# The residual add of a fused attention and fp8-linear block, moved from GpSimd's arithmetic to an accumulating DMA

## The chip, the cores and the metric

The kernel runs on one core of a Trainium2 chip. The metric is the device time in microseconds, the median of three runs; lower is better. The engines are TensorE (PE in the profile; PEld its weight loads), VectorE (DVE), ScalarE (ACT), GpSimd (POOL) and SyncE (SP), which here only issues DMAs.

## What is computed

The input x is 8 x 2048 x 512, in fp32. Attention runs over the first axis: each of the 2048 positions is a batch entry of its own with 8 tokens, 16 heads of 32.

```
xn   = layernorm(x)                                 # over the last axis
q, k, v = xn @ Wqkv.T + bqkv
attn = softmax(mask + scale * q k^T) v @ Wproj.T + bproj
lin  = fp16(fp8(xn)) @ fp16(fp8(Wffn)).T + bffn     # rounded to fp8 first
out  = x + attn + lin
```

The mask blocks keys so that queries 0 to 3 see keys 0 to 3 alone, and queries 4 to 7 see all eight.

## The kernel before

The rows are cut into 128 tiles of 128 positions x 512 numbers: tile t is token t % 8 of one half of a block of positions. Eight tiles in a row share one set of keys and values. Tiles with t % 8 below 4 are light (four keys), the others heavy (eight keys). The work is a pipeline written out by hand: in slot s each engine does stage L of tile s - L, with the stage numbers in one list (L_NORM = 3, L_KV = 4, L_Q = 5, L_QK = 8, L_SOFT = 10, L_PV = 11, L_SUM = 12, L_SPLIT = 13, L_LIN = 14, L_PROJ = 15). Each engine runs its own stream in order; semaphores alone tie the streams. The last ten tiles or so are written out apart, in `ending()` of each engine.

What each engine does in a slot, in its order, as far as the change touches it:

- PE: projection of tile s-15 into `proj_ps` (L942, then twelve matmuls of L909), the fp8 linear of s-14 (L951), the keys, values and queries of s-4 and s-5 (L909, twelve matmuls each). That is 53 matmuls. The keys wait for the transposed tile `xT`.
- DVE: statistics of a freshly loaded x (L1235), the sum of the weighted values `o_nat` (L1244), which waits for POOL's products, then query times keys (L1151), its reduction (L1156), the softmax sum and its reciprocal (L1164, L1167).
- POOL: probabilities (L513), the first four keys' weighted values `prod_pv` (L550), the shift (L521), the low half of o (L527), 1/sigma (L576), the low half of the normalised x (L581), the other four keys' weighted values if the tile is heavy (L550), the first key's product of a heavy tile (L534), and at the end of the slot the residual add of tile s-15 (L540).
- ACT: among others it scales the projection out of PSUM into `projected` (L729), rounds the linear part (L735) and presets `proj_ps` with it (L741) for the next tile.
- SP, one queue in order: the load of a new x (L364), the second fetch of x into `xs` for the residual (L386, after the store that freed the buffer has landed), the transpose of o (L396, after L527), the transposes of the fp8 x (L404) and of the fp16 x (L410, after L581), and the store of `xs` (L427, after L540).

The residual add waits for ACT's `projected` and for the second fetch of x. `projected` has one place, so ACT's next L729 waits for the add:

```
after(pool, proj_scaled, tile_count(i, n))
after(pool, res_loaded[n % 4], 16 * ring_count(i, n, 4))
nc.gpsimd.tensor_tensor(xs[:, n % 4, :], xs[:, n % 4, :], projected[:, :],
                        ALU.add).then_inc(y_ready, 1)
```

Tiles 0 to 119 take this path; for tiles 120 to 127 DVE adds the projection itself (`late_sum`, L1290).

Of the kernel before, what the change touches and what calls it, by code (L numbers as in the profile page):

```python
# [10 lines left out]
ALU = mybir.AluOpType  # L11
# [22 lines left out]

L_STATS, L_CENTRE, L_NORM, L_KV, L_Q, L_FIRST, L_QK, L_SHIFT, L_SOFT, L_PV, L_SUM, L_RES, L_SPLIT, L_LIN, L_PROJ = \
    1, 2, 3, 4, 5, 7, 8, 9, 10, 11, 12, 12, 13, 14, 15
XT, OT, PRODS = 4, 2, 4

def units_before(n):  # L40
# [23 lines left out]
def tile_count(i, n):  # L64
    return i * PAIR + (n + 1)
# [35 lines left out]

def summed_turn(t):
    return SUMMED.index(t) + 1

def live(i, j, lag):
# [17 lines left out]
def attention_and_fp8_linear(nc, x, Wqkv, bqkv, Wproj, bproj, Wffn, bffn, out):  # L124
# [3 lines left out]
    with ExitStack() as ctx:  # L128
        def sb(name, shape, dt):
            return ctx.enter_context(nc.sbuf_tensor(name, shape, dt))  # L130
# [4 lines left out]
        def sem(name):  # L135
            return ctx.enter_context(nc.semaphore(name))
# [37 lines left out]
        x8 = sb("x8", [P, 2, C], FP8)  # L174

        xT = sb("xT", [P, XT, 2 * KC, P], F16)
        xT8 = sb("xT8", [P, PAIR, KC // 2, P], F16)
        kv = sb("kv", [P, 2 * 2 * N * C], F32)
        k_all = kv[:, 0:2 * N * C].rearrange("p (g m c) -> p g m c", g=2, m=N)

# [13 lines left out]
        o_nat = sb("o_nat", [P, 2, C], F32)  # L194
        o16 = sb("o16", [P, 2, 2 * C], F16)
        oT = sb("oT", [P, OT, 2 * KC, P], F16)
        projected = sb("projected", [P, C], F32)

        k_ps, v_ps, lin_ps, proj_ps = (bank(n) for n in ("k_ps", "v_ps", "lin_ps", "proj_ps"))
        q_ps = tuple(bank(f"q_ps{k}") for k in range(4))  # L200
# [89 lines left out]
        o_lo_ready = sem("o_lo_ready")  # L290
        proj_summed = sem("proj_summed")
        proj_scaled = sem("proj_scaled")
        y_ready = sem("y_ready")

        o_turned_sum, late_hi_ready, o_rest_ready, late_lo_ready, minus_ident_ready = (
            sem(n) for n in ("o_turned_sum", "late_hi_ready", "o_rest_ready", "late_lo_ready", "minus_ident_ready"))
# [63 lines left out]
        def _(sp):  # L360
# [17 lines left out]
            def slot(i, j):  # L378
                if live(i, j, 0) and i * PAIR + j >= 4:
                    n = j  # L380
                    after(sp, x_lo_ready, tile_count(i, n - 4))
                    load_x(i, n)
                if live(i, j, L_RES):
                    n = j - L_RES
                    after(sp, y_stored[n % 4], 16 * (ring_count(i, n, 4) - 1))
                    sp.dma_start(xs[:, n % 4, :],  # L386
                                 x_v[n % N, i + n // PAIR, (n // N) % 2]).then_inc(res_loaded[n % 4], 16)
                if at(i, j, L_SPLIT):
                    sp.wait_ge(v_bias_projected, 1)
                if live(i, j, L_SPLIT):  # L390
                    n = j - L_SPLIT
                    after(sp, o_lo_ready, tile_count(i, n))
                    sp.sem_inc(o_split_seen, 1)
                    after(sp, proj_summed, tile_count(i, n - OT))
                    sp.sem_inc(oT_free_seen, 1)
                    sp.dma_start_transpose(oT[:, n % OT, :, :], o16[:, n % 2, :]).then_inc(oT_moved[n % OT], 16)  # L396
                if live(i, j, L_NORM):
                    n = j - L_NORM
                    after(sp, x_hi_q_ready, tile_count(i, n))
                    sp.sem_inc(x_hi_q_seen, 1)  # L400

                    after(sp, lin_summed, tile_count(i, n - 12))
                    sp.sem_inc(xT8_free_seen, 1)
                    sp.dma_start_transpose(xT8[:, n % PAIR, :, :],  # L404
                                           x8[:, n % 2, :].bitcast(F16)).then_inc(xT8_moved[n % 2], 16)
                    after(sp, x_lo_ready, tile_count(i, n))
                    sp.sem_inc(x_lo_seen, 1)
                    after(sp, q_summed, tile_count(i, n - XT))
                    sp.sem_inc(xT_free_seen, 1)
                    sp.dma_start_transpose(xT[:, n % XT, :, :], x16[:, n % 2, :]).then_inc(xT_moved[n % XT], 16)  # L410
                if at(i, j, L_KV):
                    sp.dma_start(wproj_nat, Wproj.rearrange("(j p) c -> p j c", p=P)).then_inc(wproj_loaded, 16)
                    with nc.allow_non_contiguous_dma(reason="512 numbers, once"):
                        sp.dma_start(v_bias_col[:, :], bqkv[2 * C:3 * C].rearrange("(k p) -> p k", p=P)).then_inc(v_bias_loaded, 16)
                    sp.dma_start(bo_all, bproj.partition_broadcast(P)).then_inc(out_biases_loaded, 16)
                    sp.dma_start(bffn_all, bffn.partition_broadcast(P)).then_inc(out_biases_loaded, 16)
                    sp.dma_start(wffn_nat.rearrange("p (j c) -> p j c", c=C),
                                 Wffn.rearrange("(j p) c -> p j c", p=P)).then_inc(wffn_loaded, 16)
                if at(i, j, 8):
                    sp.wait_ge(wffn_joined, 2)  # L420
                    for o in range(KC):
                        sp.dma_start_transpose(wffn_q[:, :, o * P:(o + 1) * P],
                                               wffn_16[:, o * C:(o + 1) * C]).then_inc(wffn_transposed, 16)
                if live(i, j, L_PROJ):
                    n = j - L_PROJ
                    after(sp, y_ready, tile_count(i, n))
                    sp.dma_start(out_v[n % N, i + n // PAIR, (n // N) % 2],  # L427
                                 xs[:, n % 4, :]).then_inc(y_stored[n % 4], 16)

            def ending():  # L430
                sp.wait_ge(x_lo_ready, TILES)
                for t in range(LATE_XS, TILES):
                    sp.dma_start(xn[:, t % 4, :], x_v[t % N, t // PAIR, (t // N) % 2]).then_inc(x_loaded[t % 4], 16)

                def load_residual(t):
                    sp.wait_ge(y_stored[t % 4], 16 * (ring_count(0, t, 4) - 1))
                    sp.dma_start(xs[:, t % 4, :], x_v[t % N, t // PAIR, (t // N) % 2]).then_inc(res_loaded[t % 4], 16)

                def store(t):
                    if t >= FIRST_LATE:  # L440
                        sp.wait_ge(late_y_ready, late_turn(t))
                    else:
                        sp.wait_ge(y_ready, t + 1)
                    sp.dma_start(out_v[t % N, t // PAIR, (t // N) % 2], late_xs(t)).then_inc(y_stored[t % 4], 16)

                def turn_o(t, count, sem_lo):
                    sp.wait_ge(sem_lo, count)
                    sp.wait_ge(proj_summed, t - OT + 1)
                    sp.dma_start_transpose(oT[:, t % OT, :, :], o16[:, t % 2, :]).then_inc(oT_moved[t % OT], 16)

                load_residual(TILES - 7)
                turn_o(TILES - 8, TILES - 7, o_lo_ready)
                store(TILES - 10)
                load_residual(TILES - 6)
                store(TILES - 9)
                load_residual(TILES - 5)
                store(TILES - 8)
                store(TILES - 7)
                turn_o(TILES - 4, 1, late_o_lo_ready)
                for t in IN_TURN[3:]:  # L460
                    store(t)
# [7 lines left out]
        def _(pool):  # L469
# [67 lines left out]
            def add_residual(i, n):  # L537
                after(pool, proj_scaled, tile_count(i, n))
                after(pool, res_loaded[n % 4], 16 * ring_count(i, n, 4))
                nc.gpsimd.tensor_tensor(xs[:, n % 4, :], xs[:, n % 4, :], projected[:, :],  # L540
                                        ALU.add).then_inc(y_ready, 1)

            def products(i, n, u, m0):
                v = v_all[:, (n // N) % 2, :, m0:m0 + 4].rearrange("p (h d) m -> p h d m", d=D)
# [100 lines left out]
        def _(act):  # L645
# [19 lines left out]
            def slot(i, j):  # L665
# [59 lines left out]
                if live(i, j, L_PROJ):  # L725
                    n = j - L_PROJ
                    after(act, proj_summed, tile_count(i, n))
                    after(act, y_ready, tile_count(i, n - 1))
                    nc.scalar.activation(projected[:, :], proj_ps[:, :], ACT.Copy,  # L729
                                         scale=out_scale[:, 0:1]).then_inc(proj_scaled, 1)  # L730
                if live(i, j, L_LIN):
                    n = j - L_LIN
# [44 lines left out]

            def scale_projected(t):
                act.wait_ge(proj_summed, t + 1)
                act.wait_ge(y_ready, t)  # L780
                nc.scalar.activation(projected[:, :], proj_ps[:, :], ACT.Copy,
                                     scale=out_scale[:, 0:1]).then_inc(proj_scaled, 1)

            def round_linear(t):
# [79 lines left out]
        def _(pe):  # L864
# [56 lines left out]
            def slot(i, j):  # L921
# [24 lines left out]
                    wait_for_lin(i, j)  # L946
                if live(i, j, L_LIN):
                    n = j - L_LIN
                    x8_pairs = xT8[:, n % PAIR, :, :].bitcast(FP8).rearrange("p j (t e) -> p j t e", e=2)
                    for c in range(KC):  # L950
                        last = nc.tensor.matmul(lin_ps[:, :], x8_pairs[:, c // 2, :, c % 2], wffn_q[:, c, :],  # L951
                                                start=c == 0, stop=c == KC - 1)
                    last.then_inc(lin_summed, 1)
# [25 lines left out]
            def late_linear(t):  # L979
                pe.wait_ge(xT8_moved[t % 2], 16 * ring_count(0, t, 2))  # L980
                pe.wait_ge(lin_rounded, turn(t) - 1)
                x8_pairs = xT8[:, t % PAIR, :, :].bitcast(FP8).rearrange("p j (t e) -> p j t e", e=2)
                for c in range(KC):
                    last = nc.tensor.matmul(lin_ps[:, :], x8_pairs[:, c // 2, :, c % 2], wffn_q[:, c, :],  # L984
                                            start=c == 0, stop=c == KC - 1)
# [367 lines left out]
```

## Time and profile before

| | |
|---|---|
| median of three runs | 1536.07 us (1536.03 to 1536.29) |
| the profiled execution's own time | 1536.16 us |
| its span, first to last instruction | 1534.4 us |
| busy: PE, PEld, DVE, ACT, POOL | 1505.7, 692.4, 1446.9, 1038.6, 1354.8 us |
| granted TensorE clock | 0.997 of full speed |
| DMA | 183 MB, mean busy share of the engines about one half |

Busy times are sums over the whole span. PE's is close to the span, but a matmul's recorded time reaches into the next one, so PE's real pace is read from the distance between starts. DMA issues are not counted as busy time of the engine that issues them.

### The profile page before, as it was taken

What the parts mean: (1) busy time and instruction counts of PE and PEld (TensorE: products, weight loads), DVE (VectorE), ACT (ScalarE), POOL (GpSimd) and SP (SyncE); (2) the same over time, 40 slices, a digit from 0 to 9 for tenths busy, and PEclk for the clock granted to TensorE, in tenths of its full rate; (3) what the DMA queues carried; (4) which work ended last, traced back from release to release, by engine and by line L of the source; (5) the groups of instructions that cost most, each with busy time, mean ns of one, the idle gap of its engine ahead of it and who ended that gap; (6) DMA issues with size and microseconds to landing.
All of it is one profiled execution on the core that took longest, in us unless ns stands there. A gap on an engine that the chain in (4) does not pass through costs nothing. (4 is left out here: it accounts for less than half of the span.)

```text
span 1534.4 us, 23337 instructions
## 1 busy us (share of the span) xinstructions
PE 1505.7 (98%) x7022; PEld 692.4 (45%) x7022; DVE 1446.9 (94%) x1220; ACT 1038.6 (68%) x2000; POOL 1354.8 (88%) x1026
## 2 busy tenths in 40 slices
PE   6999999999999999999999999999999999999997
PEld 3444444444444444444444444444444444444455
DVE  6999999999999999999999999999999999999995
ACT  5676766767766767666767666776666767667642
POOL 2579999999899989999999899989999999899983
PEclk9999999999999999999999999999999999999999
DMA  7444554545445455554545455554554545455332
GB/s 225 89 100 104 132 117 110 135 110 130 119 113 124 117 130 115 127 119 113 132 110 136 115 115 128 114 130 108 129 119 113 130 115 135 112 115 125 94 104 62
DMA packets 362350, 182.98 MB, mean 119 GB/s; under 512 B 310000, under 2 KB 310000, under 8 KB 362224
## 3 DMA queue, kind: packets, MB, share of 16 engines
q1 hardware_dynamic: 362224, 181.49, 49.6%
q8 instruction: 56, 0.92, 0.3%
q14 instruction: 70, 0.57, 0.1%
HBM read 73.41 MB, written 33.55 MB: 70 GB/s over the span
## 5 line engine op out<-in xcount | busy, mean ns | idle before, releaser
L550 POOL TENSOR_TENSOR prod_pv<-kv,probs 128x2048 f32<-128x2048 f32 x182 | 662.8, 3642 | 9.5
L1156 DVE TENSOR_REDUCE scores<-prod_qk 128x64 f32<-128x2048 f32 x192 | 439.3, 2288 | 6.8 <-DVE prod_qk L1151 0.2
L1244 DVE TENSOR_REDUCE o_nat<-prod_pv 128x512 f32<-128x2048 f32 (+1 forms) x121 | 404.6, 3344 | 40.9 <-POOL prod_pv L550 23.4
L1151 DVE TENSOR_TENSOR prod_qk<-q_ps,kv 128x1536 f32<-128x1536 f32 (+1 forms) x192 | 397.9, 2073 | 0.2 <-issue 0.2
L909 PE MATMUL k_ps<-wqkv_hi,xT 128*128 128x512 f16 x1024 | 326.2, 380 | 3.8 <-DMA xT<-x 3.2
L909 PE MATMUL v_ps<-wqkv_hi,xT 128*128 128x512 f16 x1024 | 325.5, 379 | 0.0
L909 PE MATMUL q_ps<-wqkv_hi,xT 128*128 128x512 f16 x1024 | 325.5, 379 | 0.0
L909 PE MATMUL proj_ps<-wproj_hi,oT 128*128 128x512 f16 x952 | 302.6, 379 | 0.0
L759 ACT ACTIVATE kv<-v_ps 128x512 f32<-128x512 f32 x128 | 142.2, 1111 | 150.7 <-PE v_ps L909 150.7
L909 PE MATMUL k_ps<-wqkv_lo,xT 128*128 128x512 f16 x512 | 194.4, 380 | 0.0
L909 PE MATMUL q_ps<-wqkv_lo,xT 128*128 128x512 f16 x512 | 194.1, 379 | 0.0
L909 PE MATMUL v_ps<-wqkv_lo,xT 128*128 128x512 f16 x512 | 194.1, 379 | 0.0
L909 PE MATMUL proj_ps<-wproj_lo,oT 128*128 128x512 f16 x476 | 180.4, 379 | 0.0
L581 POOL TENSOR_TENSOR x<-xn,x 128x512 f16<-128x512 f32 x128 | 149.5, 1168 | 13.0 <-ACT x L723 13.0
L909 PEld LDWEIGHTS k_ps<-wqkv_hi,xT 128*128 128x128 f16 x1024 | 100.2, 98 | 133.6 <-DMA xT<-x 15.4
L909 PEld LDWEIGHTS q_ps<-wqkv_hi,xT 128*128 128x128 f16 x1024 | 100.1, 98 | 120.9
L909 PEld LDWEIGHTS v_ps<-wqkv_hi,xT 128*128 128x128 f16 x1024 | 100.2, 98 | 120.7
L540 POOL TENSOR_TENSOR xs<-xs,projected 128x512 f32<-128x512 f32 x120 | 152.8, 1274 | 0.0
L534 POOL TENSOR_TENSOR prod_qk<-q_first,kv 128x512 f32<-128x512 f32 x64 | 81.6, 1274 | 72.5 <-DVE scores L1156 72.5
L909 PEld LDWEIGHTS proj_ps<-wproj_hi,oT 128*128 128x128 f16 x952 | 93.1, 98 | 112.4
L527 POOL TENSOR_TENSOR o<-o_nat,o 128x512 f16<-128x512 f32 x121 | 140.2, 1159 | 0.0
L663 ACT ACTIVATE q_ps<-q_bias 128x512 f32<-128x512 f32 x128 | 77.1, 603 | 91.3 <-DVE prod_qk L1151 88.8
(173 smaller groups left out, 1981.9 us busy)
## 6 DMA issues: line engine op xcount, KB each, us to landing
xn<-in_L_attn_x SPq DMA_DIRECT2D x132, 256.0 KB, 2.9
xs<-in_L_attn_x SPq DMA_DIRECT2D x124, 256.0 KB, 2.6
out<-xs SPq DMA_DIRECT2D x124, 256.0 KB, 2.1
xT<-x SPq DMA_TRANSPOSE x256, 3.0
kv<-in_L_attn_Wqkv SPq DMA_DIRECT2D x3, 1024.0 KB, 8.1
oT<-o SPq DMA_TRANSPOSE x122, 3.2
kv<-in_L_attn_Wproj SPq DMA_DIRECT2D x1, 1024.0 KB, 6.1
prod_pv<-in_L_ffn_weight SPq DMA_DIRECT2D x1, 1024.0 KB, 9.8
```

The lines of the kernel that those rows point to most:

```text
L527: nc.gpsimd.tensor_tensor(o16[:, n % 2, C:2 * C], o_nat[:, n % 2, :], o16[:, n % 2, 0:C], ALU.subtract).then_inc(o_lo_ready, 1)
L534: nc.gpsimd.tensor_tensor(prod_qk[:, 0, :], q_first[:, :], k_all[:, (n // N) % 2, 0, :], ALU.mult).then_inc(first_key_multiplied, 1)
L540: nc.gpsimd.tensor_tensor(xs[:, n % 4, :], xs[:, n % 4, :], projected[:, :], ALU.add).then_inc(y_ready, 1)
L550: nc.gpsimd.tensor_tensor(o, v, p, ALU.mult).then_inc(pv_multiplied, 1)
L581: nc.gpsimd.tensor_tensor(x16[:, n % 2, C:2 * C], xn[:, n % 4, :], x16[:, n % 2, 0:C], ALU.subtract).then_inc(x_lo_ready, 1)
L663: nc.scalar.activation(q_ps[n % 4][:, :], q_bias[:, :], ACT.Copy).then_inc(q_preset, 1)
L759: nc.scalar.activation(v_all[:, g % 2, :, n % N], v_ps[:, :], ACT.Copy).then_inc(v_kept, 1)
L909: last = nc.tensor.matmul(acc[:, :], t[:, tc, :], w[:, c, col:col + 512], start=first and k == 0, stop=k == len(parts) - 1, skip_group_che ...
L1151: nc.vector.tensor_tensor(prod_qk[:, 1:1 + m0 + 4 - m1, :], qb, k, ALU.mult).then_inc(qk_multiplied, 1)
L1156: nc.vector.tensor_reduce(scores[:, n % 2, :, m0:m0 + 4].rearrange("p h m -> p m h"), prod_qk[:, row:row + 4, :].rearrange("p m (h d) -> p ...
L1244: nc.vector.tensor_reduce(o_nat[:, n % 2, :], prod_pv[:, place:place + units, :].rearrange("p q (c m) -> p c q m", m=4), AX_XY, ALU.add).t ...
```

## The change

The residual add of tiles 0 to 119 is no longer a tensor operation on GpSimd. GpSimd issues a DMA from `projected` to `xs` that adds what it carries to what stands there. Its landing, no longer an engine's semaphore, tells SP that the store may go, and ACT that a place of `projected` is free. `projected` gets a second place. The room for it (2 KB in each partition) comes from `xT8`, the turned fp8 tiles, which shrink from 16 places to 12; the wait that guards them was for the tile twelve back already. All other instructions, orders and waits are as before.

```diff
-XT, OT, PRODS = 4, 2, 4
+XT, XT8, OT, PRODS = 4, 12, 2, 4
...
-        xT8 = sb("xT8", [P, PAIR, KC // 2, P], F16)
+        xT8 = sb("xT8", [P, XT8, KC // 2, P], F16)
...
-        projected = sb("projected", [P, C], F32)
+        projected = sb("projected", [P, 2, C], F32)
...
-        y_ready = sem("y_ready")
+        y_added = [sem(f"y_added{k}") for k in range(2)]
...
-                    after(sp, lin_summed, tile_count(i, n - 12))
+                    after(sp, lin_summed, tile_count(i, n - XT8))
...
-                    after(sp, y_ready, tile_count(i, n))
+                    after(sp, y_added[n % 2], 16 * ring_count(i, n, 2))
...
-                nc.gpsimd.tensor_tensor(xs[:, n % 4, :], xs[:, n % 4, :], projected[:, :],
-                                        ALU.add).then_inc(y_ready, 1)
+                nc.gpsimd.dma_start(xs[:, n % 4, :], projected[:, n % 2, :],
+                                    accum_op=ALU.add).then_inc(y_added[n % 2], 16)
...
-                    after(act, y_ready, tile_count(i, n - 1))
-                    nc.scalar.activation(projected[:, :], proj_ps[:, :], ACT.Copy,
+                    after(act, y_added[n % 2], 16 * (ring_count(i, n, 2) - 1))
+                    nc.scalar.activation(projected[:, n % 2, :], proj_ps[:, :], ACT.Copy,
```

`scale_projected` and `store` of the ending change in the same way, and PE reads `xT8` at the tile's number modulo 12.

## Rows read from the trace of the kernel before

**Rows 1.** The page: busy us of each engine, share of the span, instructions.
```profile
PE 1505.7 (98%) x7022; PEld 692.4 (45%) x7022; DVE 1446.9 (94%) x1220; ACT 1038.6 (68%) x2000; POOL 1354.8 (88%) x1026
```

**Rows 2.** Windows of 92 us: busy PE, PEld, DVE, ACT, POOL, clock, DMA share, GB/s.
```profile
600.00:692.00 92.00, 91.91 (x427) 41.47 (x425) 88.56 (x73) 64.34 (x125) 85.66 (x65) 1.00 0.51 121
```

**Rows 3.** PE's line L942, once a tile, and two starts in its timeline.
```profile
L942 PE MATMUL proj_ps<-out_bias_rows,ones x118: 378/379/380, 116.0 to 1460.7; 128*128 128x512 bf16 x118
...
115.95 0.38 PE L942 MATMUL proj_ps<-out_bias_rows,ones 128*128 128x512 bf16 x1
...
127.39 0.38 PE L942 MATMUL proj_ps<-out_bias_rows,ones 128*128 128x512 bf16 x1
```

**Rows 4.** Waits over the whole span: us in total, times, longest.
```profile
ACT projected L729 <- POOL xs L540: 33.5, 28, 3.1
...
PEld k_ps L909 <- DMA xT<-x: 15.4, 27, 1.2
```

**Rows 5.** POOL's timeline: its waits in eight tiles, and adds eight tiles apart.
```profile
666.91 1.28 POOL L534 TENSOR_TENSOR prod_qk<-q_first,kv 128x512 f32<-128x512 f32 x1 [2.63 <-DVE scores L1156]
...
694.66 0.41 POOL L513 TENSOR_TENSOR probs<-exps,inv_sum 128x128 f32<-128x128 f32 x1 [1.20 <-DVE inv_sum L1167]
...
705.36 1.27 POOL L540 TENSOR_TENSOR xs<-xs,projected 128x512 f32<-128x512 f32 x1
...
726.73 1.27 POOL L534 TENSOR_TENSOR prod_qk<-q_first,kv 128x512 f32<-128x512 f32 x1 [1.20 <-DVE scores L1156]
727.95 1.28 POOL L540 TENSOR_TENSOR xs<-xs,projected 128x512 f32<-128x512 f32 x1
...
746.47 1.28 POOL L534 TENSOR_TENSOR prod_qk<-q_first,kv 128x512 f32<-128x512 f32 x1 [0.71 <-DVE scores L1156]
...
819.75 1.28 POOL L540 TENSOR_TENSOR xs<-xs,projected 128x512 f32<-128x512 f32 x1
```

**Rows 6.** DVE's timeline around its one longer wait of those tiles.
```profile
715.20 0.68 DVE L1235 BATCH_NORM_STATS2 stats<-xn 128x6 f32<-128x512 f32 x1
717.55 4.42 DVE L1244 TENSOR_REDUCE o_nat<-prod_pv 128x512 f32<-128x4096 f32 x1 [1.67 <-POOL prod_pv L550]
```

**Rows 7.** SP's timeline of one slot, and the key matmul that its transpose feeds.
```profile
706.65 0.35 SPq L427 DMA_DIRECT2D out<-xs  x1
707.04 0.43 SPq L364 DMA_DIRECT2D xn<-in_L_attn_x  x1
710.92 0.33 SPq L386 DMA_DIRECT2D xs<-in_L_attn_x  x1
712.24 1.24 SPq L396 DMA_TRANSPOSE oT<-o  x1
...
715.01 1.23 SPq L410 DMA_TRANSPOSE xT<-x  x1
...
718.47 0.39 PE L909 MATMUL k_ps<-wqkv_hi,xT 128*128 128x512 f16 x1
```

**Rows 8.** What the SP queue waited for: us in total, times, longest.
```profile
SPq L393 <- POOL o L527: 358.0, 120, 6.3
SPq L427 <- POOL xs L540: 196.0, 103, 3.7
```

**Rows 9.** DMA issues by line: count, KB each, median us to landing.
```profile
xn<-in_L_attn_x SPq DMA_DIRECT2D x132, 256.0 KB, 2.9
...
out<-xs SPq DMA_DIRECT2D x124, 256.0 KB, 2.1
```

**Rows 10.** POOL's group of the add: busy us, mean ns, idle before.
```profile
L540 POOL TENSOR_TENSOR xs<-xs,projected 128x512 f32<-128x512 f32 x120 | 152.8, 1274 | 0.0
```

**Rows 11.** Timeline where the ending begins, on DVE and ACT.
```profile
1451.52 4.42 DVE L1244 TENSOR_REDUCE o_nat<-prod_pv 128x512 f32<-128x4096 f32 x1 [1.97 <-issue]
...
1459.23 0.32 ACT L681 ACTIVATE exps<-shifted,exp_scale 128x64 f32<-128x64 f32 x1
...
1460.37 0.21 DVE L1164 TENSOR_REDUCE row_sum<-exps 128x16 f32<-128x64 f32 x1
```

More of the change, by code:

```diff
@@ L103, in summed_turn, with tile @@
     return SUMMED.index(t) + 1
+def tile(i, n):
+    return i * PAIR + n
 def live(i, j, lag):
@@ L400, in slot @@
                     sp.sem_inc(x_hi_q_seen, 1)
-                    after(sp, lin_summed, tile_count(i, n - 12))
+                    after(sp, lin_summed, tile_count(i, n - XT8))
                     sp.sem_inc(xT8_free_seen, 1)
-                    sp.dma_start_transpose(xT8[:, n % PAIR, :, :],
+                    sp.dma_start_transpose(xT8[:, tile(i, n) % XT8, :, :],
                                            x8[:, n % 2, :].bitcast(F16)).then_inc(xT8_moved[n % 2], 16)
@@ L442, in store @@
                     else:
-                        sp.wait_ge(y_ready, t + 1)
+                        sp.wait_ge(y_added[t % 2], 16 * ring_count(0, t, 2))
                     sp.dma_start(out_v[t % N, t // PAIR, (t // N) % 2], late_xs(t)).then_inc(y_stored[t % 4], 16)
@@ L779, in scale_projected @@
                 act.wait_ge(proj_summed, t + 1)
-                act.wait_ge(y_ready, t)
-                nc.scalar.activation(projected[:, :], proj_ps[:, :], ACT.Copy,
+                act.wait_ge(y_added[t % 2], 16 * (ring_count(0, t, 2) - 1))
+                nc.scalar.activation(projected[:, t % 2, :], proj_ps[:, :], ACT.Copy,
                                      scale=out_scale[:, 0:1]).then_inc(proj_scaled, 1)
@@ L948, in slot @@
                     n = j - L_LIN
-                    x8_pairs = xT8[:, n % PAIR, :, :].bitcast(FP8).rearrange("p j (t e) -> p j t e", e=2)
+                    x8_pairs = xT8[:, tile(i, n) % XT8, :, :].bitcast(FP8).rearrange("p j (t e) -> p j t e", e=2)
                     for c in range(KC):
@@ L981, in late_linear @@
                 pe.wait_ge(lin_rounded, turn(t) - 1)
-                x8_pairs = xT8[:, t % PAIR, :, :].bitcast(FP8).rearrange("p j (t e) -> p j t e", e=2)
+                x8_pairs = xT8[:, t % XT8, :, :].bitcast(FP8).rearrange("p j (t e) -> p j t e", e=2)
                 for c in range(KC):
```

## The prediction, written before the result was known

> **What bounds the kernel now.** I read the page first, for the shares, then windows of the steady stretch, then distances between starts in the timelines, then the waits, and last the ending. PE is busy 98% of the span and DVE 94% [rows 1], and in a steady window of 92 us PE is busy 91.91, DVE 88.56 and POOL 85.66 [rows 2]. Nothing has much room, so the shares decide little: the question is which pace is the slowest.
>
> PE's own pace is the distance of two undisturbed starts of its once-a-tile matmul, 127.39 - 115.95 = 11.44 us [rows 3], 91.52 us for eight tiles. Its real mean is (1460.7 - 116.0) / 117 = 11.493 us [rows 3]. So from tile 0 to tile 117 PE loses 0.053 x 117 = 6.2 us and no more. The waits name the loss: the key matmuls and their weight loads wait for the DMA that turns x, 15.4 us in 27 pieces of PEld, most of which matmuls in flight cover [rows 4].
>
> Who makes the turned x late? Pattern work repeats every eight tiles (four light, four heavy). The add at 727.95 comes again at 819.75 [rows 5]: POOL's pattern takes 91.80 us, 0.28 more than PE needs. In those eight tiles POOL waits four times, always for DVE: 2.63, 1.20, 1.20 and 0.71, 5.74 us in all [rows 5]. DVE waits long once, 1.67 us at 717.55, for POOL's products [rows 6]. So the pattern's length is one loop: DVE without a gap for seven slots, its reciprocal releases POOL at 694.66, POOL runs on without a gap through the products that end at 717.3, and DVE goes on at 717.55 [rows 5, 6]. In that POOL stretch lies exactly one residual add, that of 705.36 [rows 5]. The loop drags PE by 0.28 us every eight tiles: 117 / 8 x 0.28 = 4.1 us of the 6.2. The other 2.1 I put down to single transposes that land late.
>
> The ending starts from the same loop: DVE waits 1.97 us until 1451.52 [rows 11] for POOL's products (the view says "issue", but the instruction is the same as in [rows 6]), and then runs nearly without a gap to about 1500, before PE closes the kernel.
>
> **The change part by part.**
>
> *Removed:* 120 adds of 1274 ns, 152.8 us of POOL [rows 10]. Only one in eight lies on the loop, and beyond 0.28 us per pattern PE's own pace is the floor.
>
> *Added on POOL:* 120 issues of an accumulating DMA. The trace has no DMA issued by POOL, so its cost c is bounded by SP's issues: a plain one of the same 256 KB takes 0.33 us, a transpose 1.24 [rows 7]. An accumulate reads two streams, so the far bound is twice the dearest issue, 2.48. It is a plain copy in form but not in work; I take the middle of the two single issues, 0.8, and keep 0.33 and 2.48 as the ends.
>
> With c = 0.8 the loop shortens by 1.27 - 0.8 = 0.47, to 91.33, under PE's 91.52. PE stops being dragged: -4.1 us. At c = 0.33 nothing more is won there; the 2.1 of late transposes could go too, since the turned x then comes ever earlier: -6.2.
>
> By the Trainium skill (DMA: Bandwidth & Descriptors, SWDGE vs HWDGE vs iDMA) accumulation is for DMAs of GpSimd alone, whose descriptors a Q7 core builds in software; its latency table (Latency and other measured facts) gives about 1 us to the first byte against 0.6 from SP. Were that 1 us all of GpSimd's cost, an estimate from the page, the loop would end at 91.53 and the sum would be nearly the same. No row of this trace can confirm it.
>
> *Ending:* between the wait for DVE before the last heavy products and 1451.52 lies one add again, so DVE starts its gapless run 0.47 earlier. The next thing to be late would be ACT's exponentials, which end at 1459.55 against DVE's use at 1460.37 [rows 11]: 0.82 of room, enough. So -0.5 (at c = 0.33: -0.8).
>
> *The landing takes the place of the add's end.* Before, SP may store 1.27 after POOL comes to the add. Now it waits c plus the transfer. A store of 256 KB lands 2.1 us after its issue, a load 2.9 [rows 9]. Bounds from POOL's start: 2.1, and 2.48 + 2.9 = 5.4. I take 3.5, so the store goes 2.2 us later. Queued behind it on SP are the load of x, the second fetch (which waits for the store to land), and the three transposes. SP waits for the low half of o 358.0 us in 120 times, 3.0 a slot [rows 8]: that wait absorbs the 2.2. Where it is short the chain is tight: turned x issued at 715.01, used at 718.47 [rows 7]. The load of x at 707.04, with 2.9 to land, is there at 709.9, and its statistics start at 715.20 [rows 6, 7, 9]: 5.3 of room. Cost: 0, and at the far bound (4.1 later) PE is shifted once by about 1.1, not in every slot, since SP's own issues and waits fill only part of a slot.
>
> *Second place for `projected`:* ACT's waits for the add, 33.5 us in 28 times [rows 4], end. ACT is not on the loop: 0. If ACT mattered anywhere, this would only help.
>
> *12 places for the fp8 tiles:* the wait for the tile twelve back is the same as before; 0. Same for the reordered semaphores.
>
> *DMA load:* one more 256 KB transfer per slot, on engines busy 0.51 of the time [rows 2]. It starts at the end of POOL's slot, where until now the store started; the store moves behind it. I add nothing, and count a fifth more late transposes (0.4) as inside the range.
>
> **Sum.** -4.1 - 0.5 = -4.6 from the profiled execution's own 1536.16 (span 1534.4 and 1.8 around it): 1531.5. The median of the runs is 0.09 lower than that execution, which changes nothing: 1531.5. With c = 0.33: 1536.1 - 7.0 = 1529.1.
>
> **The rivals.**
>
> *Nothing measurable (c between about 1.05 and 1.5).* At c = 1.24, the transpose's price, the loop gains 0.03. At 1.5 it loses 0.23 x 14.6 = 3.4. Half way stand -1 to +2 us, 1536. For it: an accumulate's issue is more like the dear row than the cheap one. Against: it moves 128 rows of 2 KB like the plain issues.
>
> *Slower: GpSimd's issue is dearer than its add.* With e = c - 1.27, each pattern is longer by e as long as only the loop's one add counts. The stretch before it, from 666.91 to the wait at 694.66, holds three adds and has 1.20 of room [rows 5], so from e = 0.4 on the price is 4e - 1.2 per pattern. At e = 0.7: 1.6 x 14.6 = 23 us, 1559. At the far bound, e = 1.21: 3.6 x 14.6 = 53, 1589. It decides from c = 1.5 on (+0.2%). For it: two streams to describe, and POOL with only 5.74 us idle in eight tiles [rows 5]. Against: SP's issues, all at or below 1.24 [rows 7]. 
>
> *Slower: the landing is late.* If the accumulate takes 7 us to land, the store goes 5.7 later, 2.7 more than SP's 3.0 of waiting [rows 8], the turned x is late by as much, and with 5.7 against 5.3 of room DVE waits for x too. PE's shift is paid once (+2.7), but the loop loses its gain, and transposes crowded by the longer transfer may cost another 2: about 1541.
>
> *The add was hidden anyway.* It ends with the first rival: 7 of 8 adds are in fact hidden, and if the 0.28 of the loop comes from elsewhere, only the ending's 0.5 is won: 1535.6.
>
> **How the numbers follow.** This measurement can tell 0.2% (3.1 us) from no change. Faster by more: 0.42 (c below about 1.0, the likeliest single case, own range 1529 to 1533). Within 0.2%: 0.26 (c of 1.05 to 1.5, and the hidden add). Slower: 0.32, of it 0.26 the dear issue and 0.06 the late landing. The range reaches from the low bound of c, 1529, into the dear issue up to e about 0.65, 1557; what is left out is the rest of that rival, about 0.13, and a little below.
>
> **What the changed profile would show.** If right: POOL's line L540 gone from its busy groups, and the distance from the work before the issue to the next probabilities (L513) about 0.8; adds eight tiles apart near 91.5; the wait of [rows 6] below 1.2; PEld's waits for the turned x well under 15.4 [rows 4]; ACT's wait for the add gone; SP's wait for o under 3.0 a slot, its wait before the store longer. The slower rival shows in that distance, above 1.5, POOL's waits of [rows 5] gone and DVE's wait for products grown. Wrong also if DMA transposes land visibly later than now, or if x's statistics start to wait for the load.

## The result, and the profile after

The changed kernel takes 1531.18 us (median of ten runs) beside 1536.28 for the kernel before on the same chips: 5.1 us less by the medians, 4.9 by the spans of the profiles. The ratio is 0.9969 with a 95% interval of 0.9959 to 0.9979. It is faster, by 0.3%. One of the ten runs, at 1534.3, stands alone; the others lie between 1531.05 and 1531.32. The forecast was 1531.5.

The page of the changed kernel, its busy times, its queues and one line of its issues:

```profile
span 1529.5 us, 23210 instructions
...
PE 1495.6 (98%) x6896; PEld 692.9 (45%) x7022; DVE 1446.7 (95%) x1220; ACT 1048.2 (69%) x2000; POOL 1313.9 (86%) x1026
...
q1 hardware_dynamic: 362224, 181.49, 49.5%
q0 software_dynamic: 17280, 31.46, 12.2%
...
xs<-projected POOLq DMA_DIRECT2D x120, 256.0 KB, 3.3
```

Beside [rows 1]: DVE does the same work in a span 4.9 us shorter. PE's 10 us less is not less work: 126 of its 7022 matmuls are missing from the records. POOL's own row falls by 41 us, and the experiments show that seven eighths of that buy nothing. Unlike SP's issues, GpSimd's 120 are in its busy time: they make 103.3 of the 1313.9 us. A new queue carries 31 MB and takes 12.2% of the 16 DMA engines' time.

PE's once-a-tile matmul over the whole span, as in [rows 3]:

```profile
L946 PE MATMUL proj_ps<-out_bias_rows,ones x118: 379/379/379, 116.0 to 1457.9; 128*128 128x512 bf16 x118
```

From 116.0 to 1457.9 PE lost 1341.9 - 117 x 11.44 = 3.4 us against its own pace, 6.2 before: 2.8 won. From 1457.9 to the end of the span stand 71.6 us, before 1534.4 - 1460.7 = 73.7 [rows 3]: 2.1 won. Together 4.9. The starts of this line, one by one, show where the losses lie. Before, 1.7 us are lost in the first 190 us and 4.6 behind them, spread over 17 tiles. Now 2.3 are lost in the first 200 us (1.2 of them in one tile, that of 185.7) and only 1.2 behind them, at 278 and at 634. So the drag of the steady stretch is gone, and the filling of the pipeline is left.

POOL's timeline, first of before (the two products around its add of 705.36), then of after (the same place, and POOL's waits as in [rows 5]):

```profile
701.76 3.64 POOL L550 TENSOR_TENSOR prod_pv<-kv,probs 128x2048 f32<-128x2048 f32 x1
...
707.07 3.64 POOL L550 TENSOR_TENSOR prod_pv<-kv,probs 128x2048 f32<-128x2048 f32 x1
```

```profile
665.00 1.27 POOL L538 TENSOR_TENSOR prod_qk<-q_first,kv 128x512 f32<-128x512 f32 x1 [2.94 <-DVE scores L1160]
...
692.76 0.40 POOL L517 TENSOR_TENSOR probs<-exps,inv_sum 128x128 f32<-128x128 f32 x1 [2.30 <-DVE inv_sum L1171]
...
699.86 3.63 POOL L554 TENSOR_TENSOR prod_pv<-kv,probs 128x2048 f32<-128x2048 f32 x1
703.44 0.85 POOL L544 DMA_DIRECT2D xs<-projected  x1
704.08 0.66 POOL L517 TENSOR_TENSOR probs<-exps,inv_sum 128x128 f32<-128x128 f32 x1
704.82 3.64 POOL L554 TENSOR_TENSOR prod_pv<-kv,probs 128x2048 f32<-128x2048 f32 x1
...
724.49 1.27 POOL L538 TENSOR_TENSOR prod_qk<-q_first,kv 128x512 f32<-128x512 f32 x1 [1.54 <-DVE scores L1160]
```

This gives the disputed price. From product to product it took 707.07 - 701.76 = 5.31 us with the add and 704.82 - 699.86 = 4.96 with the issue: GpSimd saves 0.35 us, not 1.27. The issue's row says 0.85; the probabilities start 0.64 after it, but last 0.66 instead of 0.41. With the add's 1.27 the price c is 0.92. POOL's whole busy time says the same: 41 us less for 120 adds is 0.34 each.

DVE's timeline: its wait for products, the same reduction eight tiles apart, and the start of its run to the end (answering [rows 6] and [rows 11]):

```profile
703.87 4.42 DVE L1248 TENSOR_REDUCE o_nat<-prod_pv 128x512 f32<-128x4096 f32 x1 [0.19 <-DVE stats L1239]
...
715.31 4.42 DVE L1248 TENSOR_REDUCE o_nat<-prod_pv 128x512 f32<-128x4096 f32 x1 [1.35 <-POOL prod_pv L554]
...
795.33 4.42 DVE L1248 TENSOR_REDUCE o_nat<-prod_pv 128x512 f32<-128x4096 f32 x1 [0.19 <-DVE stats L1239]
...
1446.61 4.42 DVE L1248 TENSOR_REDUCE o_nat<-prod_pv 128x512 f32<-128x4096 f32 x1 [1.62 <-issue]
```

The pattern of eight tiles takes 795.33 - 703.87 = 91.46 us, where [rows 5] had 91.80, so it lost 0.34, the saving of one add and not of eight. Over the 14.6 patterns of the steady part this is 0.34 x 14.6 = 5.0, and DVE's last run starts 4.91 us earlier (1451.52 to 1446.61). From there to the end both kernels take 82.9 us.

The waits, PE's weight loads first, then ACT's and SP's, beside [rows 4] and [rows 8]:

```profile
PEld k_ps L913 <- DMA xT<-x: 7.1, 10, 1.5
...
ACT projected L733 <- PE proj_ps L913: 35.3, 78, 2.7
...
SPq L431 <- DMA xs<-projected: 467.1, 118, 6.1
...
SPq L398 <- POOL o L531: 103.4, 89, 6.8
```

The weight loads' wait is halved. ACT waits for PE's result instead of POOL's add. SP now spends 467.1 us before its stores, 4.0 a slot, and its wait for the low half of o fell from 358.0 to 103.4: the later landing was taken out of that wait.

### The profile page after: what moved, and what is told of

The parts are those of the page before. It is cut to its first block, busy times and chain, and to the rows that moved or that the text cites. A ratio compares the mean times of both kernels' runs of the same rounds, so it can differ in the third digit from the quotient of the medians.

```text
span 1529.5 us, 23210 instructions
## 1 busy us (share of the span) xinstructions
PE 1495.6 (98%) x6896; PEld 692.9 (45%) x7022; DVE 1446.7 (95%) x1220; ACT 1048.2 (69%) x2000; POOL 1313.9 (86%) x1026
## 3 DMA queue, kind: packets, MB, share of 16 engines
q1 hardware_dynamic: 362224, 181.49, 49.5%
q0 software_dynamic: 17280, 31.46, 12.2%
## 4 chain that ended last, share of the span: by engine, by line
PE 74%; POOL 5%; issue 4%; DVE 2%; DMA 1%; SPq 0%; ACT 0%; POOLq 0%; DVEq 0%
PE k_ps L913 17%; PE v_ps L913 17%; PE q_ps L913 16%; PE proj_ps L913 16%; PE lin_ps L955 5%; POOL prod_pv L554 2%; PE proj_ps L946 1%; DVE prod_qk L1155 1%; DVE scores L1160 1%; POOL prod_pv L613 1%; POOL x L585 1%; DMA xT<-x 1%; POOL o L531 1%; POOL xs L544 0%; PE q_ps L1030 0%
## 5 line engine op out<-in xcount | busy, mean ns | idle before, releaser
L752 ACT ACTIVATE kv<-k_ps 128x512 f32<-128x512 f32 x128 | 76.3, 596 | 135.6 <-PE k_ps L913 135.6
L733 ACT ACTIVATE projected<-proj_ps,out_scale 128x512 f32<-128x512 f32 x118 | 80.4, 681 | 35.3 <-PE proj_ps L913 35.3
```

Of the source, the lines that this page charges most:

```text
L733: nc.scalar.activation(projected[:, n % 2, :], proj_ps[:, :], ACT.Copy, scale=out_scale[:, 0:1]).then_inc(proj_scaled, 1)
L752: nc.scalar.activation(k_all[:, g % 2, n % N, :], k_ps[:, :], ACT.Copy).then_inc(k_kept, 1)
```

## The experiments

### Which adds count, and what the places do

Three kernels split the change. Each has the two places of `projected` and the 12 of `xT8`; they differ in `by_dma`.

```diff
-                nc.gpsimd.dma_start(xs[:, n % 4, :], projected[:, n % 2, :],
-                                    accum_op=ALU.add).then_inc(y_added[n % 2], 16)
+                if by_dma(tile(i, n)):
+                    nc.gpsimd.dma_start(xs[:, n % 4, :], projected[:, n % 2, :],
+                                        accum_op=ALU.add).then_inc(y_added[n % 2], 16)
+                else:
+                    nc.gpsimd.tensor_tensor(xs[:, n % 4, :], xs[:, n % 4, :], projected[:, n % 2, :],
+                                            ALU.add).then_inc(y_ready, 1)
```

`by_dma` is `t % 8 == 2` (the 15 adds on the loop), `t % 8 != 2` (the other 105) or never.

> Only the adds of tiles with t % 8 == 2 (one in eight, the one that lies between DVE's release of POOL and the products that DVE waits for) go by DMA; the other seven stay on GpSimd; two places as in the changed kernel. The loop theory: nearly the whole gain is there, 1531 to 1532.5, with fewer late transposes because only 15 accumulating transfers run. The theory that all of POOL's time counts: one eighth of the 5.1, 1535.5. The theory that the second place for the projection made the gain: 1531 as well, which the kernel with two places alone tells apart.

> The complement: all adds by DMA except those of tiles with t % 8 == 2. The loop theory: the steady part gains nothing from POOL, and the ending's add on the loop stays too: 1535 to 1536.5. The theory that all of POOL's time counts: seven eighths of the gain, 1531.8.

> Every add stays on GpSimd as before; only the second place for the scaled projection (and 12 places for the fp8 tiles) is kept. The loop theory: ACT is not on the loop, so 1536 within 0.5. The theory that ACT's 33.5 us of waiting for the add mattered: 1531 to 1533, with no DMA at all.

| adds issued as DMA | median us | ratio to before, 95% interval |
|---|---|---|
| 15, those on the loop | 1531.24 | 0.9967 [0.9955, 0.998] |
| 105, all others | 1536.52 | 1.0002 [0.9993, 1.0011] |
| none, only the places | 1536.25 | 1.0000 [0.9991, 1.0009] |
| all 120 (the change) | 1531.18 | 0.9969 [0.9959, 0.9979] |

All three came out inside what was expected. Fifteen adds bring the whole gain; the other 105, which relieve POOL by seven times as much, bring nothing, nor do the places. The wait for the turned x, in the kernel with 15 and in that with 105:

```profile
PEld k_ps L938 <- DMA xT<-x: 6.7, 10, 1.4
```

```profile
PEld k_ps L938 <- DMA xT<-x: 13.8, 18, 1.8
```

With 15 DMAs it is as short as with all 120, with 105 nearly as long as before [rows 4]. So the turned x came late because the loop pushed it, not because of the DMA engines' load. The 105 aren't free for PE, though: its matmuls wait 6.1 us for the turned x, 3.2 before, and its last once-a-tile matmul starts at 1462.1 instead of 1460.7. The time doesn't show this. DVE's last run starts at 1451.86, and from there to the end it takes 82.8 us, as in the kernel before: the end hangs on DVE, not on PE.

### Give the saved time back

Behind each DMA issue of the changed kernel two small GpSimd operations on idle data fill the stretch up to the old length.

```diff
                 nc.gpsimd.dma_start(xs[:, n % 4, :], projected[:, n % 2, :],
                                     accum_op=ALU.add).then_inc(y_added[n % 2], 16)
+                nc.gpsimd.tensor_tensor(spare[:, :], ident[:, 0:64], ident[:, 0:64], ALU.add, saturate=False)
+                nc.gpsimd.tensor_tensor(bqkv_nat[:, :], ident[:, 0:12], ident[:, 0:12], ALU.add)
```

> The changed kernel, with two small idle additions on GpSimd (128 x 64 and 128 x 12) behind each DMA issue, about 0.4 us together, so that the add costs GpSimd as much as the tensor operation did (0.92 + 0.4 against 1.27), while everything else of the change stays. The loop theory, as the first runs leave it (the whole 4.9 us of span is 0.35 us of GpSimd's time in 14 patterns of eight tiles): all of the gain goes, 1536 to 1538. A theory by which the freed order of SP and ACT behind the add gave part of it: 1532 to 1534.

Measured: 1537.23 us, 1.0008 [0.9999, 1.0017]. Its timeline, product to product:

```profile
702.16 3.63 POOL L557 TENSOR_TENSOR prod_pv<-kv,probs 128x2048 f32<-128x2048 f32 x1
...
707.50 3.64 POOL L557 TENSOR_TENSOR prod_pv<-kv,probs 128x2048 f32<-128x2048 f32 x1
```

That is 5.34 us, 0.03 above the kernel before, and the gain is gone. So GpSimd's saved 0.35 us is the cause, and not the new path of `projected`, the moved store or SP's waits, which this kernel has too. It is 0.97 us above before, and that too is the loop's: DVE's pattern of eight tiles takes 91.85 us, 0.06 more than before (0.06 x 14.6 = 0.9), and its last run starts 0.92 later. PE's last once-a-tile matmul starts 3.6 us later than before (1464.3), which costs nothing beyond that: again the end hangs on DVE.

### The other direction: the add twice

A second GpSimd add of the same operands, into a spare tile; all else as before, but for the 12 places of `xT8`.

```diff
                 after(pool, res_loaded[n % 4], 16 * ring_count(i, n, 4))
+                nc.gpsimd.tensor_tensor(spare[:, :], xs[:, n % 4, :], projected[:, :], ALU.add)
                 nc.gpsimd.tensor_tensor(xs[:, n % 4, :], xs[:, n % 4, :], projected[:, :],
```

> The kernel before with a second addition of the same size in front of each residual add (its result goes nowhere), so that c rises by 1.22 us. The price formula of the prediction (three adds in the stretch before, with 1.20 of room, and one on the loop: 4e - 1.2 for each pattern) gives 3.7 x 14.6 = 54, 1590. If only the loop's one add ever counted: 1.22 x 14.6 = 18, 1554. If all eight counted: 142, 1678.

Measured: 1594.58 us, 1.038 [1.0366, 1.0394], so 58.3 us, 4.6 above the 1590 of the formula; one add and eight adds at full price are both far off. DVE's pattern takes 95.74 us (two of its reductions, eight tiles apart, start at 728.71 and 824.45), 3.95 more than before, for e = 1.22, the distance between the two adds' starts. The formula says 3.68 there. POOL's wait for query times keys, before and here, shows what the formula lacks:

```profile
POOL prod_qk L534 <- DVE scores L1156: 72.5, 45, 3.8
```

```profile
POOL prod_qk L535 <- DVE scores L1158: 5.5, 3, 3.8
```

From 661 to 860 us POOL's timeline in this kernel has no wait at all. POOL had 5.74 us of idle time in eight tiles [rows 5] and got eight second adds: 8 x 1.22 - 5.74 = 4.02 per pattern, 58.7 over 14.6 patterns. So at this price all eight adds count, less the idle time, and POOL's whole work sets the pace. This price passes 4e - 1.2 at e = 1.14. Whether 4e - 1.2 holds for a smaller e, no run shows. Had the issue cost twice SP's dearest, e = 1.21, the kernel would be about 57 us slower by this estimate.

### One place, and the landing's wait on ACT

The accumulating DMA reads the one place too, and `scale_projected` of the ending changes in the same way.

```diff
-                    after(act, y_added[n % 2], 16 * (ring_count(i, n, 2) - 1))
-                    nc.scalar.activation(projected[:, n % 2, :], proj_ps[:, :], ACT.Copy,
+                    if tile(i, n) >= 1:
+                        act.wait_ge(y_added[(n - 1) % 2], 16 * ((tile(i, n) - 1) // 2 + 1))
+                    nc.scalar.activation(projected[:, 0, :], proj_ps[:, :], ACT.Copy,
```

> The changed kernel with a single place for the scaled projection: ACT waits for the landing of the tile before. The loop theory: ACT is not on the loop; a landing comes 3.3 us after the issue and ACT has had waits of up to 3.1 us at this line before, so 1531 to 1533. If the second place is needed as soon as the add is a DMA, because ACT's waits reach the presets of the linear part and the keys: 1534 and more.

Measured: 1531.34 us, 0.997 [0.9959, 0.9982]. ACT does wait:

```profile
ACT projected L734 <- DMA xs<-projected: 62.3, 31, 4.8
...
ACT projected L786 <- DMA xs<-projected: 6.0, 1, 6.0
```

In the steady part 62.3 us of waiting, up to 4.8 at once, cost nothing: PE's last once-a-tile matmul starts at 1457.9, as in the changed kernel. ACT has a third of its time free. In the ending it can cost something: the wait of 6.0 us (L786 is `scale_projected`) stands in the profiled execution's chain, where a landing of 4.64 us releases ACT at 1477.37 and ACT releases PE at 1478.90, and this execution is 1.0 us longer than the changed kernel's. Four of the six executions take 1531.0 to 1531.4, two 1532.3 and 1532.7. So the second place isn't needed for the gain; it may be worth 1 us in some executions.

### No add at all

> The add is left out of tiles 0 to 119 (their output is x alone); SP stores when ACT has scaled the projection, POOL pays nothing (c = 0), and no accumulating transfer runs. It gives the floor of what any way of doing the add can win. The loop theory: PE at its own pace of 11.44 us a tile, the late transposes of the start gone as well, and the ending a little earlier: 1528.5 to 1530. If POOL's 0.92 us of issue still costs in the changed kernel beyond the loop, the floor is much lower, 1525 or less.

Measured: 1525.55 us, 0.993 [0.9916, 0.9943]. The expectation was missed by 3 us, and the result lies near the 1525 of the other reading, that GpSimd's 0.92 us still costs beyond the loop; the kernel after this one decides between them. PE's once-a-tile matmul tells where the 3 us are:

```profile
L952 PE MATMUL proj_ps<-out_bias_rows,ones x118: 379/379/379, 116.0 to 1455.4; 128*128 128x512 bf16 x118
```

The steady part is 2.5 us shorter than in the changed kernel (1455.4 against 1457.9), and the ending is 1523.8 - 1455.4 = 68.4 instead of 71.6. I had taken the ending to be PE's, with only tenths to win. It isn't: in the changed kernel the chain of work that ended last (start, us, what) runs through PE up to 1398, whose pace is within 0.06 us a pattern of the loop's, and from there to 1504 through POOL and DVE.

```profile
1418.04 3.63 POOL prod_pv L554
...
1450.95 2.29 DVE prod_qk L1155
...
1464.81 2.30 DVE scores L1160
...
1499.43 4.37 DVE o_nat L1320
```

DVE brings to the ending what the loop between it and POOL gained in the whole kernel; PE, held at its own pace of 91.52 per pattern, can't. From the start of DVE's last run to the end of the span it is 82.8 to 83.0 us in the kernel before, in the changed one, in the three that split it and in the padded one, wherever PE stands. Without any add DVE's run starts at 1439.13 and the end comes 84.7 later: now the chain runs through PE.

### The add off the loop without any DMA

If it is the place of one add in eight that costs, then that add need not become a DMA; it can run one slot later, behind the products that DVE waits for. All 120 adds are again GpSimd's. Only for t % 8 == 2 (the last is t = 114) the add, its store and the next fetch into the same buffer move one slot.

```diff
+def late_add(t):
+    return t % 8 == 2 and t < TILES - 10
...
-                    add_residual(i, j - L_PROJ)
+                    t = tile(i, j - L_PROJ)
+                    if late_add(t - 1):
+                        add_residual(0, t - 1)
+                    if not late_add(t):
+                        add_residual(0, t)
```

> No DMA add at all. All adds are tensor operations on GpSimd, with two places for the projection, and the add of tiles with t % 8 == 2 is done one slot later, behind the products that DVE waits for (its store and the second fetch into its buffer move by a slot too). The loop then holds no add, c = 0 for it, with GpSimd's total work as before. The loop theory: better than the changed kernel, near the kernel without any add (1525.6) until GpSimd's next stretch or PE takes over: 1526 to 1529. The theory that GpSimd's total time counts: 1536, as before. If SP's two stores in a row make the turned x late: 1533 to 1538.

Measured: 1526.21 us, 0.9935 [0.9922, 0.9947], the fastest complete kernel of this study, 5.0 us under the changed one and 0.7 above the kernel without any add. So of what leaving out all 120 adds wins, moving 15 of them wins nearly all. Its timeline on POOL, then on DVE, and its once-a-tile matmul:

```profile
697.87 0.41 POOL L551 TENSOR_TENSOR probs<-exps,inv_sum 128x128 f32<-128x128 f32 x1
698.36 3.64 POOL L592 TENSOR_TENSOR prod_pv<-kv,probs 128x2048 f32<-128x2048 f32 x1
...
704.97 3.63 POOL L592 TENSOR_TENSOR prod_pv<-kv,probs 128x2048 f32<-128x2048 f32 x1
708.57 2.49 POOL L582 TENSOR_TENSOR xs<-xs,projected 128x512 f32<-128x512 f32 x2
```

```profile
708.84 4.42 DVE L1290 TENSOR_REDUCE o_nat<-prod_pv 128x512 f32<-128x4096 f32 x1 [0.43 <-POOL prod_pv L592]
```

```profile
L988 PE MATMUL proj_ps<-out_bias_rows,ones x118: 379/379/379, 115.9 to 1456.0; 128*128 128x512 bf16 x118
```

No add stands between the products of 694.28 and 698.36; two stand together at 708.57, and DVE starts its reduction while they run. POOL is as busy as in the kernel before (1355.7 us), and waits now for ACT, whose work hangs on PE's:

```profile
POOL x L623 <- ACT x L769: 33.5, 46, 1.8
...
POOL o L565 <- ACT o L750: 28.5, 29, 1.3
```

PE loses 1340.1 - 1338.5 = 1.6 us in the steady part, in two tiles, those of 150.2 and 173.9, and its ending takes 68.3. In this kernel's chain nothing but PE stands from 178.46 to 1486.96; behind that it is PE with five pieces of ACT, 0.7 us at most, and DVE's last 0.75.

### Both: late add, and the rest by DMA

The kernel above with `by_dma` for `t % 8 != 2`.

> On top of the kernel whose add of every eighth tile is moved one slot back, the other 105 adds are issued as accumulating DMAs, so that GpSimd's timeline loses 105 times about 0.35 us. If only the add on the loop between GpSimd and VectorE ever cost time, this is worth nothing and the accumulating transfers make single turned tiles late: 1526 to 1527.5 us, with more waits of PEld for the turned x than without them. If GpSimd's total work still counts once the loop is free of the add, 37 us less of it show: 1525 us or less.

Measured: 1528.42 us (1528.06 to 1529.72), 0.9947 [0.9934, 0.9961]. It is 2.2 us slower than the kernel above, by medians beside 1536.31 and 1536.26 for before, and no run of one reaches the other's. Relieving POOL by 105 x 0.35 = 37 us has a negative worth. The loss is larger than expected, and the profiled execution (span 1527.9, 3.6 above the kernel without DMAs) has all of it in one place. The timelines there, with the DMAs and without:

```profile
175.24 0.88 POOL L579 DMA_DIRECT2D xs<-projected  x1
176.05 1.73 SPq L445 DMA_TRANSPOSE xT<-x  x1
...
180.33 0.39 PE L955 MATMUL k_ps<-wqkv_hi,xT 128*128 128x512 f16 x1 [2.52 <-DMA xT<-x]
...
181.24 0.63 PE L955 MATMUL k_ps<-wqkv_lo,xT 128*128 128x512 f16 x1
...
181.67 0.63 PE L955 MATMUL k_ps<-wqkv_hi,xT 128*128 128x512 f16 x1
```

```profile
175.34 1.23 SPq L445 DMA_TRANSPOSE xT<-x  x1
...
178.46 0.39 PE L955 MATMUL k_ps<-wqkv_hi,xT 128*128 128x512 f16 x1 [0.69 <-DMA xT<-x]
```

The transpose is issued 0.71 later and takes 4.2 instead of 3.1 to let PE go on, with an accumulating transfer issued 0.8 ahead of it; PE starts 1.87 later. Why it is issued later stands in the chain (start, us, what):

```profile
165.81 4.89 DMA xs<-projected
...
170.72 2.04 DMA out<-xs
...
172.78 0.33 SPq L415
```

The accumulating transfer lands after 4.89 us, only then SP stores, and behind that store's landing stand the second fetch (L415) and the transposes. So here the landing, which cost nothing in the steady stretch, is on the path to PE. Behind the wait PE's matmuls start 0.43 apart, twice the usual 0.22. The windows of this kernel behind its wait (busy PE, PEld, DVE, ACT, POOL, clock, DMA share, GB/s):

```profile
180.50:184.00 3.50, 3.50 (x10) 1.27 (x9) 3.43 (x5) 0.72 (x2) 3.50 (x4) 0.53 0.81 198
184.00:200.00 16.00, 16.00 (x76) 7.21 (x74) 15.65 (x14) 10.70 (x21) 14.49 (x13) 1.00 0.78 149
```

The granted clock fell to 0.53 for 3.5 us, about the lower level of 1.2 GHz, after PE had waited 2.52 us for the turned tile: another 1.7 us. Together 3.6, as the distances between PE's once-a-tile starts say: this tile takes 4.38 us over PE's own pace, without DMAs 0.86. The Trainium skill (TensorE: Matmul & The Clock Gate, Part 1: The HAM clock gate) says that a gate halves the array's clock after it has had little to do and gives it back under load; the rows agree. The other four executions are 1.2 to 1.7 us shorter than the profiled one and had a mean granted clock of 0.998 instead of 0.997, so they probably lacked the fall of the clock. They are 1.9 to 2.3 us above the kernel without DMAs, about the 1.9 of the late transpose alone; that they lose it in the same place isn't shown.

## Why the prediction was right, point by point

**The bound and the loop: right.** The loop between DVE and POOL with one add per eight tiles was the cause; 15 adds bring the gain, 105 bring nothing, padding takes it away, and moving one add per pattern takes the place of the DMA. The rival "the add was hidden anyway" falls with the result of 15 adds.

**The price c: mis-sized, without effect.** Taken 0.8, measured 0.92: the saving is 0.35 and not 0.47, and DVE's wait for the products came to 1.35, where one below 1.2 was to be the sign. Since the loop came to 91.46, just under PE's 91.52, the term of the steady part would have been the same. It was taken from SP's issues for want of a row of POOL's, and lies between the two single ones, nearer the dear one. The issue also lengthened the operation behind it, which the row of the issue doesn't show. The rival "dear issue" is refuted in its condition (c of 1.5). Its price at the far bound was too low: 4e - 1.2 leaves out that POOL has only 5.74 us of idle time in eight tiles, and the doubled add measured 3.95 per pattern where it gives 3.68. The Trainium skill's rule on which it leaned (GPSIMD Engine Reference, When to use GPSIMD), one core for read and one for write descriptors, might still hold; a doubling for the second stream isn't seen in the rows, 0.85 beside SP's 0.33 and 1.24. Nor is its opposite shown, since no plain DMA was issued by GpSimd.

**The sum: right, its two terms wrong.** "-4.1 - 0.5" was measured as -2.8 and -2.1. One term was 1.3 too large and the other 1.6 too small, so that the sum comes within 0.3 of the measured 4.9 is in part luck. The steady term was too large: I took all that remained after the drag, 2.1, for single late transposes that the change would leave alone, and 3.4 remained, 2.3 of it in the first tiles, while the pipeline fills. The rest is two pieces of the changed kernel's chain (start, us, what):

```profile
278.15 4.52 DMA xT<-x
...
633.96 3.90 DMA xT<-x
```

An accumulating DMA was issued at 277.22, just ahead of the first, and at 634.23, just behind the start of the second. That these made the transposes late is possible, by the longest landing of that transpose line (5.4 us; 4.8 before and 4.4 in the kernel with the late add), but every slot has such a pair, and it wasn't tried alone. The ending term was too small: I gave it only the saving of the last pattern's add. The step that failed is "beyond 0.28 us per pattern PE's own pace is the floor": true for PE until 1457.9, not for DVE and POOL, who carry the whole 4.9 into an ending that hangs on them. The kernel with 105 DMAs and the padded one show it: PE comes 1.4 and 3.6 us later than before to its last once-a-tile matmul, DVE 0.3 and 0.9 later to its last run, and the time follows DVE. Had the loop been cut deeper, as in the late add, the forecast would have been wrong by this: 5 us more were to be had, of which the floor allowed none but the late transposes.

**The landing takes the place of the add's end: right for this change.** 3.3 us against 3.5 taken; SP's wait for o absorbed it (358.0 to 103.4), and the x whose load SP issued at 707.71 is there 2.7 later, 2.9 ahead of its statistics at 713.28 (5.3 before), so DVE's waits for it stay at 1.7 us in all. A landing can take more, 5.4 at most in the changed kernel, and where one took 4.9 while the pipeline filled, in the last kernel, it was on the path to PE. The Trainium skill (DMA: Bandwidth & Descriptors, Anatomy of one DMA) fits a GpSimd DMA with 2.0 us and 436 GB/s, an estimate of 2.6 for 256 KB; measured from issue to landing are 3.3 for the accumulating one. The Trainium skill (Perfetto Trace Analysis, DMA Instruction, SWDGE) says that the profile's end of such an instruction is that of its descriptors, not of its data; the rows agree, 0.85 beside 3.3.

**The second place, the 12 places, the semaphores at nothing: right**, by the kernel with the places alone and, but for up to 1 us in the ending of some executions, by that with one place.

**DMA load at nothing: right in size for the change, wrong in kind.** It costs something, seen once the loop is out of the way: 2.2 us for 105 transfers. How much of that is the DMA engines' load and how much the later landing in front of SP's store, the two kernels don't tell apart.

What stays open: how much of the lateness of single transposes comes from the accumulating transfers, where the last kernel loses its 2.2 us in the executions without a profile, and whether a GpSimd DMA without accumulation would cost less.

## What to carry to other kernels

Before taking work off a busy engine, find the loop of waits between the two busiest ones and count how many of the operations lie on it: here 15 of 120. Then ask first whether that one can stand elsewhere in the same engine's order, since moving it gained twice as much as handing all 120 to the DMA, without a new transfer. And read the ending as a kernel of its own: an engine held at a floor in the steady part gives no floor to the others, who bring their gain to the end.

## What the runs showed of the hardware

- An accumulating DMA of 128 x 2 KB costs GpSimd 0.92 us: 0.64 until its next operation starts, and that one, of 0.41, takes 0.66. Two small operations behind it (128x64, 128x12) and the probabilities took from 706.38 to 707.50 in the padded kernel.
- 120 such transfers of 256 KB take 12.2% of the DMA engines' time for 31 MB, while 181 MB of the other queue take 49.5%: 0.39% per MB against 0.27%.
- With these transfers beside it the DMA transpose that feeds PE has a longer tail. In the kernels with the late add its landings (least, median, most) are, without and with 105 of them (in the kernel before, without any, the most is 4.8):

```profile
DMA to landing us min/median/max: 3.0/3.1/4.4
```

```profile
DMA to landing us min/median/max: 3.0/3.4/5.6
```

- One wait of PE of 2.5 us, in a stretch where it was otherwise busy, was followed by 3.5 us at a granted clock of 0.53: PE started 1.9 us later than in the kernel without DMAs, and the lower clock cost 1.7 more. In the changed kernel a wait of 1.04 us, at 190.59, was followed by no fall: the granted clock was 1.00 from 190 to 194.
